# All transfers of the third stage issued by SyncE in one queue

## The reference

```python
def layer(x, ctx, w1, b1, w2, b2):              # x, ctx: 32 x 512 x 512
    kv = ctx * ctx
    r[t] = 0.9 * r[t - 1] + kv[t]               # scan over the rows of a batch
    x2 = x + layernorm(x) * r
    y = layernorm(x2)
    yq, s1 = quantize(y)                        # uint8, ONE scale: the maximum of all of y
    h = relu(yq @ int8(w1).T + bias1)           # 512 -> 2048 columns
    hq, s2 = quantize(h)                        # uint8, ONE scale: the maximum of all of h
    return x2 + hq @ int8(w2).T + bias2         # 2048 -> 512 columns
```

## Time and profile before

| | us |
|---|---|
| median of 3 runs | 1276.0 (1275.71 to 1276.96) |
| the profiled execution | 1276.56 |
| its span in the profile | 1274.8 |
| PE busy | 1216.2 (95%) |
| ScalarE busy | 980.4 (77%) |
| DVE busy | 871.2 (68%) |
| mean DMA rate over the span | 352 GB/s |

### The profile page before, as it was taken

The page is one execution under the profiler, slowest core; times in us unless marked ns, Lnnn a source line. Parts: engine busy times, 40 slices in busy tenths (PEclk is TensorE's granted clock), DMA queues, the critical chain, the costliest instruction groups (busy, mean ns, idle before and its releaser), DMA issues. The chain is left out here.

```text
span 1274.8 us, 15533 instructions
## 1 busy us (share of the span) xinstructions
PE 1216.2 (95%) x5386; PEld 561.0 (44%) x5386; DVE 871.2 (68%) x1262; ACT 980.4 (77%) x1211; POOL 162.3 (13%) x394
## 2 busy tenths in 40 slices
PE   5998999998799999999999999799999999999998
PEld 2444444443344444444444444344444444434343
DVE  4887999886577777777777777564565554444456
ACT  4788899886677777777777776788788777777794
POOL 2655546544000000000000000000000000000000
PEclk9999999999799999999999999899999999999999
DMA  9999999971377899999999988599999999999996
GB/s 354 404 399 342 391 350 342 355 260 66 159 303 286 312 414 401 366 362 354 352 355 364 358 334 353 204 365 418 416 417 416 417 416 417 417 418 415 417 363 232
DMA packets 134614, 448.78 MB, mean 352 GB/s; under 512 B 10740, under 2 KB 10760, under 8 KB 123400
## 3 DMA queue, kind: packets, MB, share of 16 engines
q1 hardware_dynamic: 82312, 273.71, 54.7%
q10 hardware_dynamic: 52224, 174.08, 37.0%
HBM read 254.81 MB, written 192.94 MB: 351 GB/s over the span
## 5 line engine op out<-in xcount | busy, mean ns | idle before, releaser
L866 PE MATMUL ps<-w2T,xq 128*128 128x512 f16 x2048 | 449.2, 380 | 12.7 <-ACT xq L586 12.3
L824 PE MATMUL ps<-xq,w1T 128*128 128x512 f16 x2048 | 448.6, 380 | 1.4 <-DVE xq L701 1.4
L586 ACT ACTIVATE xq<-xq,hb,hs 128x512 f16<-128x512 f32 x494 | 357.5, 801 | 83.1 <-PE ps L866 70.7
L692 DVE TENSOR_REDUCE work<-xq 128x2 f32<-128x1024 f32 x255 | 311.1, 1220 | 125.7 <-ACT xq L535 125.7
L535 ACT ACTIVATE xq<-ps 128x1024 f32<-128x1024 f32 x255 | 260.9, 1023 | 123.1 <-PE ps L824 122.8
L866 PEld LDWEIGHTS ps<-w2T,xq 128*128 128x128 f16 x2048 | 198.9, 98 | 263.0 <-ACT xq L586 27.4
L802 PE MATMUL ps<-xq,work 128*128 128x512 f32 x640 | 283.0, 603 | 24.8 <-ACT xq L469 24.8
L824 PEld LDWEIGHTS ps<-xq,w1T 128*128 128x128 f16 x2048 | 199.3, 98 | 236.7 <-issue 1.8
L802 PEld LDWEIGHTS ps<-xq,work 128*128 128x128 f32 x640 | 122.7, 193 | 178.2 <-issue 161.2
L740 DVE TENSOR_TENSOR work<-ps,cs_bc 128x512 f32<-128x512 f32 x128 | 86.9, 690 | 89.4 <-PE ps L866 82.9
L751 DVE SCALAR_TENSOR_TENSOR work<-work,nmean,bq_bc 128x512 f32<-128x512 f32 x96 | 65.7, 747 | 82.5 <-DMA work<-x_scratch 82.4
(11 more groups left out here) (99 smaller groups left out, 455.2 us busy)
## 6 DMA issues: line engine op xcount, KB each, us to landing
hidden_scratch<-xq SPq DMA_DIRECT2D x240, 512.0 KB, 6.0
xq<-hidden_scratch ACTq DMA_DIRECT2D x220, 512.0 KB, 19.8
xq<-in_ctx_dram ACTq DMA_DIRECT2D x31, 1024.0 KB, 9.5
xq<-in_x_dram SPq DMA_DIRECT2D x24, 1024.0 KB, 11.9
x_scratch<-xq SPq DMA_DIRECT2D x24, 1024.0 KB, 8.3
out_dram<-work SPq DMA_DIRECT2D x24, 1024.0 KB, 14.8
work<-x_scratch SPq DMA_DIRECT2D x22, 1024.0 KB, 8.0
work<-x_scratch ACTq DMA_DIRECT2D x21, 1024.0 KB, 8.3
```

Source lines behind the costliest of these rows:

```text
L586: act.activation(hq[c % HQ], src[:, c % 2, :], ACT.Relu, bias=hb[:, q:q + 1], scale=hs[:, q:q + 1]).then_inc(h_scaled, 1)
L692: dve.tensor_reduce(hmax[:, b * NF + 2 * q:b * NF + 2 * q + 2], src, AX.X, ALU.max).then_inc(kept_maxed, 1)
L824: last = pe.matmul(bank, w1T[:, k, f * P:(f + 1) * P], xq_rows(b, k), start=(k == 0), stop=(k == KD - 1))
L866: last = pe.matmul(acc_bank(s, i), src[:, i * P:(i + 1) * P], w2T[:, q, :], start=first, stop=final)
```

## The change

ScalarE no longer issues any transfer in the third stage. SP issues all of them, in one order written out by pairs: at each pair of the 256 it may first store a turn's output (turn `s` at pair `17 + 8 s`, `OUT_AT`), then load the `x2` of turn `s + 4` (at pair `28 + 8 s`, `OUT_AT + XBACK`), and then issue the hidden load that the pair's scaling makes room for. The waits ahead of each transfer are those of before.

```diff
--- before.py
+++ after.py
@@ -43,6 +43,8 @@
 NXQ = 3
 NKEEP = 12
 XC = 4
+OUT_AT = 17
+XBACK = 11
 NX = 3
 NPAIR = 3
 NTURN = 3
@@ -361,14 +363,27 @@
             for n in range(NKEEP):
                 sp.wait_ge(h_stored[n], 16 * stores_in(n))
             sp.wait_ge(kept_maxed, NLOAD)
+
+            def load_kept(c):
+                if c >= NKEEP:
+                    sp.wait_ge(h_scaled, 2 * (c - NKEEP + 1))
+                sp.dma_start(hload[c % NRING].rearrange("p n t -> p (n t)"), h_dram[c // NP2, c % NP2]).then_inc(h_loaded[c % NRING], 16)
+
             for c in range(NKEEP):
-                sp.dma_start(hload[c].rearrange("p n t -> p (n t)"), h_dram[c // NP2, c % NP2]).then_inc(h_loaded[c], 16)
+                load_kept(c)
             for s in range(HELD, XC):
                 load_x2c(s)
-            for s in range(len(turns_c) - 1):
+            for pair in range(len(copied) * NP2):
+                s, after = divmod(pair - OUT_AT, NP2)
+                if after == 0 and 0 <= s < len(turns_c) - 1:
+                    store_out(s)
+                s, after = divmod(pair - OUT_AT - XBACK, NP2)
+                if after == 0 and 0 <= s and s + XC < len(turns_c):
+                    load_x2c(s + XC)
+                if NKEEP <= pair + NKEEP < NLOAD:
+                    load_kept(pair + NKEEP)
+            for s in range((len(copied) * NP2 - 1 - OUT_AT) // NP2 + 1, len(turns_c) - 1):
                 store_out(s)
-                if s + XC < len(turns_c):
-                    load_x2c(s + XC)
 
             last = len(turns_c) - 1
             for i in range(NI):
@@ -562,10 +577,6 @@
                         load_x2(t + 2)
 
 
-            def load_kept(c):
-                act.wait_ge(h_scaled, 2 * (c - NKEEP + 1))
-                act.dma_start(hload[c % NRING].rearrange("p n t -> p (n t)"), h_dram[c // NP2, c % NP2]).then_inc(h_loaded[c % NRING], 16)
-
             act.wait_ge(h_scales, 1)
             for c in range(len(copied) * NF):
                 q = c % NF
@@ -584,8 +595,6 @@
                         act.wait_ge(h_loaded[n % NRING], 16 * (n // NRING + 1))
                     src = hload[n % NRING]
                 act.activation(hq[c % HQ], src[:, c % 2, :], ACT.Relu, bias=hb[:, q:q + 1], scale=hs[:, q:q + 1]).then_inc(h_scaled, 1)
-                if c % 2 == 1 and NKEEP <= pair + NKEEP - 1 < NLOAD:
-                    load_kept(pair + NKEEP - 1)
 
 
         @block.vector
```

## The result

| | before | after |
|---|---|---|
| median of 5 runs, us | 1276.64 (1275.71 to 1277.96) | 1270.41 (1269.48 to 1270.99) |
| profiled execution, us | 1276.56 | 1270.41 |
| its span, us | 1274.8 | 1268.6 |

What follows compares the result with a forecast made beforehand. PE, busy 95%, loses time in the third stage waiting for ScalarE, whose issues stall on a full DMA queue. Forecast: 1276.56 - 6.0 = 1270.6, median of runs 0.56 lower, so 1270.0 us; range 1265.0 to 1278.5.

Steps and rivals of the forecast that it cites:

- ScalarE issues nothing: Third stage: 228 issues leave ScalarE, removing the 10.3 us that PE waits for it after 1040 us.
- most that can be won: 10.3 us: Upper bound from PE's waits for ScalarE in 1040 to 1220 us; the span would end at 1264.5.
- SP in the full queue harms nobody: SP issues the 228 loads at 0.32 to 0.64 us each; when it stalls, only later transfers wait behind it.
- The hidden loads stay ahead: Near the end of the third stage, hidden loads land 9 us ahead of need, so PE never waits for them.
- The x2 load of turn 29 sets the end: Load lands at 1242.0, DVE needs 26.8 us more: span ends at 1268.8, 6.0 us earlier.
- the two ways of reckoning: Landing of turn 29's x2 load: 1239 by mean DMA rate, 1242 from the old kernel's end; 1242.0 was taken.
- The rest: Time from the landing of turn 29's x2 load to the end of the span: 33.3 - 6.5 = 26.8 us.
- One queue carries as much: One queue in place of two loses no bandwidth: 422 GB/s seen in one queue against 416 to 417 in two.
- Rival D: Slower: the single queue has gaps behind x2 loads or stores; 1283 at 0.5 us a turn, 1296 at 1; chance 0.17.
- Rival B: The x2 load lands early enough (1239 or sooner): gain 9 to 10.3 us, 1265.7 to 1267; chance 0.18.
- The waits of PE for DVE: PE may wait about 1 us for a bank at the start of turn 31, at no extra cost.
- Rival C: No change: DMA bounds the stage and the stall only moves; 1273.4 to 1278.6 us, chance 0.18.

Runs made afterwards that it cites:

- pool_h: The kernel before, with GpSimd instead of ScalarE issuing the 228 hidden loads, SP's old loop kept: 1271.90 us, ratio 0.9959.
- quarter: The kernel before, each turn's store writing only the first of its four blocks, ScalarE issuing as ever: 1262.95 us, ratio 0.9889.
- XBACK 1 and 3: The changed kernel with 1 or 3 instead of 11 pairs between a slot's store and its next x2 load: 1345.81 and 1311.12 us, one run each.
- xback14: The changed kernel with 14 instead of 11 pairs between a slot's store and its next x2 load: 1272.09 us, ratio 0.9959.
- xback8: The changed kernel with 8 instead of 11 pairs between a slot's store and its next x2 load: 1268.94 us, ratio 0.9933.
- xback5: The changed kernel with 5 instead of 11 pairs between a slot's store and its next x2 load: 1268.18 us, ratio 0.9927.
- tail5: The changed kernel with distance 5 for the last four x2 loads only (turns 28 to 31), 11 for the others: 1269.03 us, ratio 0.9937.
- tail_order: `xback5` with the stores of turns 27 and 28 moved ahead of the x2 loads of turns 30 and 31: 1267.64 us, ratio 0.9929.
- act_late: The changed kernel with the later half of the hidden loads (pairs 112 to 227) given back to ScalarE: 1287.25 us, ratio 1.0085.
- pool_x2: The changed kernel with the 28 x2 loads issued by GpSimd in a queue of their own: 1267.74 us, ratio 0.9930.

## Why the prediction held

The time (1270.41 for 1270.0) and the mechanism were right; two terms were off, and part of the closeness is luck: the stage gained 2.0 us more than forecast, and began 1.8 us later.

1. **ScalarE issues nothing.** Right in kind: `pool_h` shows the gain with two queues and the old order, `quarter` shows that a queue with room makes the same issues free. The size "most that can be won: 10.3 us" was too small. The runs show 14.4. I had taken PE's idle rows for its whole loss. The forecast did not suffer, since another term decided.
2. **SP in the full queue harms nobody.** Right: SP's issues of up to 5.95 us hold no engine that computes, though they grew long before the "about 1000" of the prediction: 3.1 us between 880 and 920, 5.6 between 920 and 960. That its wait for a store is harmless too was right only with five or more hidden loads behind the store.
3. **The hidden loads stay ahead.** Right: ScalarE waits for no load after the change. With XBACK 1 and 3 it does (97.8 and 67.8 us from 840 us on), since the rate itself falls.
4. **The x2 load of turn 29 sets the end.** Right, and the deciding term. I had it used at 1242.0, which is 434.2 us into the stage, and it came at 432.6, between the two ways of reckoning (431.2 and 434.2). The rest was put at 26.8 and took 26.4. So the stage gained 8.0 us where I had 6.0, and the profiled execution lost 1.8 us of it ahead of the stage. In `xback14` and `xback8` this load moves and the end follows. In `xback5` and `tail5` it comes so early that the x2 load of turn 31 takes its place.
5. **One queue carries as much.** Right at XBACK 11: 415 to 418 GB/s. Rival D's mechanism, a single queue that stands still behind a store, is real: it needs the wait too close to the store.

Rival B's bound (1264.5, a stage of 456.7 us) is not PE's: `tail_order` goes below it with 455.8, and `quarter` takes 452.6. In every changed version that writes the whole output, but for `act_late`, an x2 load of the last turns set the end; in `act_late` and in the kernel before it was PE, late by ScalarE's issues. The waits of PE for DVE were put at about 1 us and are 2.3 us in six pieces; they cost nothing extra, as the prediction says. Rival C fell with the ratio's interval. That DVE's wait of some 7 us a turn costs nothing until the last turns was implied, and `tail5` shows it.

## What to carry to other kernels

An engine that feeds the critical one should not issue into a queue that can be full: look at the duration of its issues over time, not at their number. When a kernel is bound by transfers, order decides which of them is late at the very end. Follow the last use of each kind back to the store or load that it waits for, and move only the last few. In a single queue, put enough work between a store and the transfer that waits for its landing: here five hidden loads (2.62 MB, 6.3 us at 416 GB/s) were enough and three (3.8 us) were not.

## What was not expected

- PE's idle rows understate a loss. In 180 us they showed 10.4 us and the count of matmuls 14.4. Count matmuls in equal windows.
- The landing of a store in a full queue takes 12 to 20 us (`xback5`, `pool_x2`); with three hidden loads behind it the rate dropped by a tenth. Why a store takes so long to land no run isolates.
- An issue of a plain load on GpSimd took 0.54 us in the median and 0.78 at most, with loads that landed in 21.8 us in the median (`pool_h`; 32.2 us in 1040 to 1220 us, and up to 38.5), so GpSimd was not held back by its queue as SP and ScalarE were by theirs. The backlog stood in the queue, and the ring of 28 places was long enough for it.
